# Moving split Q and K between two SBUF layouts: a trip through DRAM against 24 short on-chip copies

## The reference

```
kqv = x @ Wqkv + bqkv ; q, k, v = its three thirds, by 16 heads of 32
scores = einsum('bsnh,btnh->bnst', k, q) / sqrt(32)        # then triangular mask
out = softmax(scores, axis=2) weighted sum of v ; x = LN(x + out @ Wo + bo)
x = LN(x + expert(x, fside, ctx))      # two "SmoothQuant" int8 products
x = LN(x + routed_and_shared_ffn(x))   # 16 experts, 4 per token, and shared ones
```

## Time and profile before

| | us |
|---|---|
| median of 3 runs | 1476.31 (1475.5 to 1485.98) |
| profiled execution, its own time | 1484.92 |
| its span in the trace | 1483.2 |
| PE busy / DVE busy / ACT busy | 1339.3 / 888.9 / 411.6 |
| first pass / three middle passes, roughly | 0 to 130 / 130 to 600 |

### The profile page before, as it was taken

How to read it: one execution, slowest core, us unless ns; L and a number is a source line. 1 busy time by engine, 2 the same in 40 slices (tenths; PEclk the granted TensorE clock), 3 DMA queues, 4 the chain that set the end, 5 groups by cost and what they waited for, 6 DMA issues and landing times.

```text
span 1483.2 us, 24661 instructions
## 1 busy us (share of the span) xinstructions
PE 1339.3 (90%) x7339; PEld 992.9 (67%) x7339; DVE 888.9 (60%) x1579; ACT 411.6 (28%) x627; POOL 389.5 (26%) x478
## 2 busy tenths in 40 slices
PE   7988998999998998789978998999999999879991
PEld 3553455445454455278857887999999999768890
DVE  2542787669856887687757876334343455555634
ACT  1132133303341144212120013223222334343423
POOL 1131012200230014000001671344444344343432
PEclk9989998999989999889998999999999999999996
DMA  8431533225420632413110012645464456868437
GB/s 283 133 89 39 156 92 96 72 87 141 114 72 23 176 100 68 154 39 131 58 57 29 29 37 66 167 77 139 77 141 75 84 133 140 236 175 237 83 72 249
DMA packets 90109, 163.96 MB, mean 111 GB/s; under 512 B 8544, under 2 KB 29536, under 8 KB 89968
## 3 DMA queue, kind: packets, MB, share of 16 engines
q1 hardware_dynamic: 73168, 122.88, 26.7%
q0 software_dynamic: 16816, 39.59, 14.4%
HBM read 113.42 MB, written 49.02 MB: 110 GB/s over the span
## 4 chain that ended last, share of the span: by engine, by line
PE 68%; DVE 11%; DMA 7%; issue 7%; ACT 2%; SPq 1%; POOL 1%; DVEq 1%; ACTq 0%; POOLq 0%
PE psUA L1001 13%; PE psUB L1001 12%; PE psR L1095 11%; PE psY L1008 9%; PE psR L1008 5%; PE psR L1171 3%; PE psOT L1202 3%; PE psST L1185 3%; PE psTX L984 2%; PE psR L1109 2%; DMA kst<-scr_d 2%; PE psTH L1017 2%; DMA room<-in_L_ffn_w_dram 2%; DMA qst<-nml 1%; DVE nm L1566 1%
## 5 line engine op out<-in xcount | busy, mean ns | idle before, releaser
L1001 PE MATMUL psUA<-w_s,xgT 128*128 (+1 forms) x1284 | 244.6, 341 | 18.8 <-DVE xgT L1379 16.1
L1001 PEld LDWEIGHTS psUA<-w_s,xgT 128*128 128x128 f32 x1284 | 214.4, 196 | 27.0 <-DVE xgT L1379 15.4
L1001 PE MATMUL psUB<-w_s,xgT 128*128 (+1 forms) x1284 | 225.3, 324 | 0.0
L1001 PEld LDWEIGHTS psUB<-w_s,xgT 128*128 128x128 f32 x1284 | 211.4, 190 | 0.0
L827 POOL DMA_INDIRECT sx_d<-yg,dst_i x74 | 119.4, 1614 | 299.3 <-ACT yg L905 261.8
L867 ACT ACTIVATE silg<-psUA 128x352 f32<-128x352 f32 x107 | 49.6, 464 | 432.8 <-PE psUB L1001 432.8
L1008 PE MATMUL psY<-w_s,hgT 128*128 (+3 forms) x621 | 163.6, 408 | 0.1
L789 POOL TENSOR_SCALAR_AFFINE_SELECT pT<-pT 128x128 f32<-128x128 f32 (+1 forms) x192 | 68.5, 375 | 347.6 <-ACT pT L943 347.5
L1388 DVE SCALAR_TENSOR_TENSOR hg<-silg,cws,psUB 128x352 f32<-128x352 f32 x75 | 43.5, 579 | 174.4 <-ACT silg L867 174.4
L1566 DVE TENSOR_REDUCE nm<-psR 128x1 f32<-128x128 f32 (+3 forms) x256 | 113.1, 486 | 41.9 <-PE psR L1173 37.5
L1008 PEld LDWEIGHTS psY<-w_s,hgT 128*128 128x128 f32 (+1 forms) x621 | 114.6, 192 | 23.0 <-DVE hgT L1396 0.5
(11 more groups left out here) (218 smaller groups left out, 1901.3 us busy)
## 6 DMA issues: line engine op xcount, KB each, us to landing
room<-in_L_ffn_w_dram SPq DMA_DIRECT2D x32, 704.0 KB
scr_d<-qhl SPq DMA_DIRECT2D x32, 512.0 KB, 3.7
qst<-scr_d SPq DMA_DIRECT2D x48, 256.0 KB, 4.0
kst<-scr_d SPq DMA_DIRECT2D x48, 256.0 KB, 5.9
room<-in_L_ffn_w_dram SPq DMA_DIRECT2D x16, 512.0 KB
xt<-in_x_dram SPq DMA_DIRECT2D x5, 1024.0 KB, 7.2
xr<-in_x_dram SPq DMA_DIRECT2D x4, 1024.0 KB, 5.5
breg<-in_fside_BxS2xS_dram SPq DMA_DIRECT2D x4, 1024.0 KB, 7.1
```

Source lines behind the costliest of these rows:

```text
L1001: mm = pe.matmul(t[:, 0:F], xgT[:, par, a_, c * P:(c + 1) * P], w[:, buf, b_, c, :], start=(c == 0 and n == 0), stop=(c == C - 1 and n == ...
```

## The change

For head groups 0 and 1 of every pass, SP no longer stores to `scr_d` and loads from it. It issues 24 DMAs of 64 KB within the chip: for each of the six blocks and each head j, 32 partitions of `qhl` go to 32 partitions of the stack. Groups 2 and 3 keep the way through `scr_d`, with the counts of `s_scr` adjusted. ACT, which before waited at `qk:2` and `qk:4` (and the K step behind each) until the two stores of the group before had landed (`s_scr`), now waits until all 24 copies of that group have landed (`s_stk`).

```diff
+        STACKED = (16 * 24, 16 * 30)
...
                         at.let_go(sp, x)
-                        for t in (2 * g, 2 * g + 1):
-                            sp.dma_start(scr_d[t].rearrange("v p s -> p v s"), qhl[:, t % 2].bitcast(F32)).then_inc(s_scr, 16)
-                        sp.wait_ge(s_scr, a * (32 * C) + 32 * (g + 1))
-                        apart(sp)
                         if g >= 2:
+                            for t in (2 * g, 2 * g + 1):
+                                sp.dma_start(scr_d[t].rearrange("v p s -> p v s"), qhl[:, t % 2].bitcast(F32)).then_inc(s_scr, 16)
+                            sp.wait_ge(s_scr, a * (32 * (C - 2)) + 32 * (g - 1))
+                            apart(sp)
 
                             sp.wait_ge(s_st, a * (2 * HEADS) + 8 * (g - 1))
                             apart(sp)
                         for t, stack, first, second in ((2 * g, qst, (0, 1), 0), (2 * g + 1, kst, (0, 0), 1)):
                             src = scr_d[t].rearrange("v (j r) s -> v r j s", r=HD)
                             for k, v in enumerate((*first, second)):
-                                sp.dma_start(stack[HD * k:HD * (k + 1), i].bitcast(F32), src[v]).then_inc(s_stk[i], 16)
+                                if g >= 2:
+                                    sp.dma_start(stack[HD * k:HD * (k + 1), i].bitcast(F32), src[v]).then_inc(s_stk[i], 16)
+                                else:
+                                    for j in range(4):
+                                        sp.dma_start(stack[HD * k:HD * (k + 1), i, j].bitcast(F32),
+                                                     qhl[HD * j:HD * (j + 1), t % 2, v].bitcast(F32)).then_inc(s_stk[i], 16)
...
                         act.wait_ge(s_rfull, at.ticket(x) + 1)
-                        if n >= 2:
-
-                            act.wait_ge(s_scr, a * (32 * C) + 32 * (n // 2))
+                        if 2 <= n < 6:
+
+                            act.wait_ge(s_stk[n // 2 - 1], a * STACKED[1] + STACKED[0])
+                        elif n >= 6:
+                            act.wait_ge(s_scr, a * (32 * (C - 2)) + 32)
...
                     elif kind == "max" and n % 4 == 0:
-                        pe.wait_ge(s_stk[n // 4 % 2], 96 * (2 * a + n // 8 + 1))
+                        pe.wait_ge(s_stk[n // 4 % 2], a * STACKED[1] + STACKED[n // 8])
```

## The result

The changed kernel takes 1525.53 us (median of 4 runs, 1517.8 to 1527.17) against 1475.9 for the kernel before. The ratio of the runs is 1.0311, with an interval of 1.0253 to 1.0369: 3.1% slower, where 1.4% was forecast. The time lies outside the stated range, by 5.5 us. In the later comparisons the kernel before took 1482 to 1485 us; so experiments are compared by their ratio to it, not by their times.

The account below looks back on a forecast made before the run. PE was busy nine tenths of the span, with the DRAM trip hidden under DVE's work in middle passes. Middle passes 17.0, first pass 2.5, group 1 0 and clock 1.5 make 21 us: 1476.31 to 1497.3 us, range 1483 to 1520.

Parts of the forecast that it names:

- The moved wait: ACT's wait at qk:2 lasts until the group lands, not the stores; 5.65 us per middle pass, 2.5 in the first.
- I take 0.47: Spacing in us of SP's 24 issues, taken from load bursts; bounds 0.36 and 0.63; the 24th starts 10.7 us after the first.
- L: Time from the end of qk:1's (or qk:3's) readout to the landing of the whole group: 12.9 us, 12.7 before.
- L - 10.4: First pass, group 0: delay of max:0 in us, 2.5 at L of 12.9.
- costs nothing at 12.9: ACT's wait for group 1's copies at qk:4 adds 0 us with L at 12.9 us.
- L - 13.6: Group 1, middle passes: qk:4 allows L up to 13.6 us, so no cost at 12.9.
- L - 13.0: Group 1, first pass: ACT's wait at qk:4 in us, just nothing at L of 12.9.
- Rival 3: Copies within the chip are dear: 0.63 us each, L 16.7, group 1 no longer hidden, together 47.6 us, 1524; chance 0.16.
- the clock: PE's idle time ahead of v:2 brings a granted clock of 1.2 GHz: 0.5 us per pass, 1.5 in all (0 to 6).
- L - 7.25: Middle passes, group 0: delay of DVE's qk:2 and of max:0, 5.65 us each, 17.0 over three passes.
- Rival 1: Transfers, not issues, set L at 8.46 us; 1479.3 us, no change that can be told; chance 0.08.
- a later wait that got shorter: Sign of being wrong in the profile: a later wait shortened by what was lost in this stretch; no size given.

Follow-up runs that it names:

- two-places run with merged copies: The changed kernel with 12 copies of 128 KB per group and group 1's qk:2 and qk:3 split into `otu`: ratio 1.000 to the kernel before.
- the run with the wait alone: The kernel before, stores and loads through DRAM kept, but ACT waits at qk:2 to qk:5 until the previous group's stack has landed: ratio 1.0117.
- the probe: The kernel before plus six bursts of six SP DMAs after its last store: 0.59 us per issue with both ends in SBUF, 0.43 with one in DRAM.
- the two-places run: The changed kernel, still 24 copies per group, with qk:2 and qk:3 split into `otu` and ACT waiting only from qk:4: ratio 1.0159 to the kernel before.
- the 12 merged copies: The changed kernel with Q's and K's blocks of a head in one copy, 12 of 128 KB per group: ratio 1.010 to the kernel before.

## Why the prediction was wrong

- **Direction and mechanism: right.** The trip through DRAM was hidden in the middle passes; the two-places run with merged copies, at 1.000, shows that taking it away gives nothing. The moved wait delays qk:2 on ACT and then everything on DVE and PE; the run with the wait alone, 1.0117, shows it.
- **The step that failed: "I take 0.47, because that is the spacing of DMAs in a burst into these same tiles".** I took the price of an issue from the nearest tile. The price depends on whether both ends lie in SBUF, as the probe shows, and the only row with that was `qst<-nml`, 0.59 us in the earlier trace rows, which I had put at the far end of the range. Measured is 0.63 with its gap, so the 24th issue starts 14.5 us after the first, not 10.7. With the landing of 2.0 us, L is 16.5 us instead of 12.9. In the terms of the forecast that is 3 x 3.6 for the middle passes and 3.6 for the first, 14.4 us too little. The first pass confirms the rule: L - 10.4 gives 6.1, measured are 6.2.
- **Group 1: mis-sized for the same reason.** That it "costs nothing at 12.9" rested on 0.7 us of cover in the middle passes and none in the first. At 16.5 the rule L - 13.6 gives 2.9 per middle pass, and L - 13.0 gives 3.5 in the first; measured were 2.6, 1.9, 2.8 and 4.3, in all 11.6 us, for a forecast of 0. With L at 16.5 the forecast's own rules add 14.4 and 12.2 us to its 21, which makes 47.6 us; the medians differ by 49.6.
- **Rival 3 named the result.** With 0.63 us an issue it gave 47.6 us and 1524; measured are 47.6 in the two columns of the trace and 1525.5. That close a match is partly luck: the rival had 34.7 us for group 0 and 13.0 for group 1 where the trace has 36.1 and 11.6, it left out the clock, and the two profiled executions differ by 40, not 47.6. I gave it a chance of 0.16 and cut the range at 1520, short of my own bound.
- **The clock: about right for this kernel, for a partly wrong reason.** 1.5 us were forecast. The delays to max:0 in the middle passes are 10.6, 10.1 and 9.2 us against the 9.25 that L - 7.25 gives, so about 2 us. My reading, not a run's, is that it is this cheap because half of the low clock falls into the wait itself: it lasts from about 191 to 201 us, and PE has nothing to do until 195.25. Where PE waits right ahead of the stretch that it shares with DVE, as in the two-places run, 3.1 us more are lost in each pass.
- **Landing of 64 KB within the chip:** 2.2 taken, 2.0 measured. **Rival 1** (transfers set L) is excluded by the 12 merged copies: same bytes, L of 10.2 instead of 16.5. Copies this small are not the usual case of the Trainium skill (DMA: Bandwidth & Descriptors, section Issuing engines are not separate DMA queues), in which the time on the sequencer to start a DMA is small relative to the DMA itself. Here one issue takes 0.59 us of the 2.0 to its landing, and SP is issuing for 15.1 of the 16.5 us.
- **What I did not foresee:** that the rest of the stage would give back some 10 us in the profiled execution. The prediction had named a later wait that got shorter as a sign of being wrong; it is not that, but where the lower clock falls, as the windows above show for the largest part. The medians, 49.6 us apart, do not show a gain.

## What to carry to other kernels

Price an issue by a row with the same kinds of ends, not by a row with the same tile, and count issues: a direct way with 24 of them was longer than a way through DRAM with 8. When a copy is made slower or later, look at who waits for its source to be free as well as who waits for its destination; here the two had about half of the loss each. With a second place for group 1 and the same 24 copies the ratio fell from 1.031 to 1.016, and what was left was the later landing and the clock behind it. And look for the place where a copy does end last before taking one away that is hidden: loading head by head, as the heads leave, gained 0.6% with the same bytes.

## What the runs showed of the hardware

A DMA issued by SP with both ends in SBUF holds the queue for 0.59 us, one with an end in DRAM for 0.43 (medians), for 64 KB and 256 KB alike; with the gap, 0.63 and 0.47 in a burst. The first of a burst can be shorter (0.55 us at 177.16). SP and ACT issue side by side and hardly slow each other (12 on ACT in 7.7 us, while SP's 12 start from 25.9 to 33.2). After 3.1 us of idle PE the granted clock was at 0.50 for about 10 us, beginning some 2 us after PE was back at work, so that the price of such a wait was nearly twice its length. It does not follow every short wait: with 12 merged copies two middle passes with almost the same idle time differed, one at 1.00 throughout and one at 0.50, and the second took 3.1 us longer.
